# Attention output on one Trainium2 core: one transposition and four 64x64 products in place of two folding products and one full product

## What is computed

```python
x = x + attn(layernorm(x))            # Wq, Wk, Wv, Wo: 128 x 128
x = x + ffn(layernorm(x))             # w_router 128 x 8, w1 8 x 128 x 512, w2 8 x 512 x 128, bias

def attn(x):                          # per head: softmax(q k / sqrt(8)) v over a window of 64
    ...
    ctx = ctx.transpose(0, 2, 1, 3).reshape(Bx, Lx, D_OUT)   # 16 heads x 8 channels side by side
    return ctx @ Wo
```

## Time and profile before

| | |
|---|---|
| three runs, median | 861.02 us (860.0 to 861.64) |
| the profiled execution, own time | 864.88 us |
| its span, first to last instruction | 863.0 us |
| mean granted TensorE clock | 0.951 of full |
| attention and routing of sequences, about | 20 to 535 us |
| experts | 600 to 863 us |
| PE busy, share of the span | 88% |
| DVE, ACT, POOL busy | 60%, 52%, 41% |

### The profile page before, as it was taken

How to read it: one execution, slowest core, us unless ns; L and a number is a source line. 1 busy time by engine, 2 the same in 40 slices (tenths; PEclk the granted TensorE clock), 3 DMA queues, 4 the chain that set the end, 5 groups by cost and what they waited for, 6 DMA issues and landing times. The chain is left out here.

```text
span 863.0 us, 19198 instructions
## 1 busy us (share of the span) xinstructions
PE 760.3 (88%) x7469; PEld 544.6 (63%) x7469; DVE 519.1 (60%) x1623; ACT 451.1 (52%) x923; POOL 357.1 (41%) x318
## 2 busy tenths in 40 slices
PE   7999999999999999999999998427999889889983
PEld 3556666666566566566666555314988778778872
DVE  7888888988888888887887887610222212211210
ACT  5576685585585585585586664202444334334421
POOL 3000000032232222322322343562877877877877
PEclk9999999999999999999999999557999999999997
DMA  4942000010110010010010011113364554554533
GB/s 137 387 160 62 8 15 8 34 33 25 50 33 21 31 47 30 22 56 30 21 57 30 21 66 40 67 51 117 32 111 59 93 101 58 96 97 59 87 31 33
DMA packets 50132, 54.21 MB, mean 63 GB/s; under 512 B 6018, under 2 KB 39449, under 8 KB 49025
## 3 DMA queue, kind: packets, MB, share of 16 engines
q0 software_dynamic: 22528, 17.22, 14.0%
q1 hardware_dynamic: 27520, 35.86, 12.6%
HBM read 17.70 MB, written 31.59 MB: 57 GB/s over the span
## 5 line engine op out<-in xcount | busy, mean ns | idle before, releaser
L445 POOL DMA_INDIRECT out<-y_sb,xg x128 | 199.2, 1556 | 71.1 <-issue 55.0
L363 POOL DMA_INDIRECT slots_dram<-send_rows,slot_id x112 | 110.3, 985 | 229.4 <-PE sT_ps L1135 163.1
L520 ACT ACTIVATE probsT<-sT_ps 128x1024 f32<-128x1024 f32 x128 | 132.4, 1035 | 60.2 <-PE sT_ps L1135 58.7
L687 DVE TRANSPOSE_TENSOR_REDUCE kmax<-sT_ps 128x32 f32<-128x1024 f32 x128 | 159.5, 1246 | 6.2 <-PE sT_ps L1118 5.7
L619 ACT ACTIVATE hT<-sT_ps 128x512 f32<-128x512 f32 x128 | 76.6, 599 | 154.7 <-PE sT_ps L1347 139.1
L1118 PE MATMUL sT_ps<-qbd,kT 64*128 64x256 f32 x1024 | 133.2, 380 | 0.0
L1347 PE MATMUL sT_ps<-xT_hl,w_hl 128*128 128x512 f32 x384 | 105.1, 426 | 24.8 <-DVE xT_hl L1045 18.5
L1055 DVE TENSOR_TENSOR y_sb<-o_ps,xg 128x256 f32<-128x256 f32 x32 | 13.6, 425 | 188.3 <-DMA out<-y_sb,xg 106.2
L1118 PEld LDWEIGHTS sT_ps<-qbd,kT 64*128 64x128 f32 x1024 | 98.6, 191 | 9.8
L1347 PEld LDWEIGHTS sT_ps<-xT_hl,w_hl 128*128 128x128 f32 x384 | 75.9, 204 | 43.9 <-DVE xT_hl L1045 19.1
L380 POOL TENSOR_TENSOR xbias<-x_sb,bias_sb 128x256 f32<-128x256 f32 x32 | 23.5, 734 | 192.8 <-PE sT_ps L1135 192.8
(11 more groups left out here) (171 smaller groups left out, 1124.7 us busy)
## 6 DMA issues: line engine op xcount, KB each, us to landing
slots_dram<-empty_rows SPq DMA_DIRECT2D x8, 1096.0 KB, 16.7
xg<-slots_dram SPq DMA_DIRECT2D x32, 274.0 KB
out<-xbias SPq DMA_DIRECT2D x32, 128.0 KB
w_sb<-in_L_ffn_w SPq DMA_DIRECT2D x16, 256.0 KB
send_rows<-rows_sb SPq DMA_DIRECT2D x7, 548.0 KB, 3.2
out<-y_sb,xg POOLq DMA_INDIRECT x128
slots_dram<-send_rows,slot_id POOLq DMA_INDIRECT x112
out<-empty_rows SPq DMA_DIRECT2D x1, 1024.0 KB, 24.4
```

Of the source, the lines that this page charges most:

```text
L363: pool.indirect_dma_start(out=slots_dram, out_offset=bass.IndirectOffsetOnAxis(ap=slots[:, k, j:j + 1].bitcast(U32), axis=0), in_=rows[:, ...
L445: pool.indirect_dma_start(out=out, out_offset=bass.IndirectOffsetOnAxis(ap=xg[:, r, 4 * c + k, ROW - 1:ROW].bitcast(U32), axis=0), in_=y_s ...
L520: nc.scalar.activation(probsT[:, gp].rearrange("p b k h q -> p (b k h q)"), sT_ps[:, gp].rearrange("p b c -> p (b c)"), ACT.Exp).then_inc( ...
L687: nc.vector.tensor_reduce(kmax[:, u % 2, :], sT_ps[:, u % 2].rearrange("p b (c q) -> p (b c) q", q=32), AX.X, ALU.max, apply_transpose=Tru ...
```

## The change

`normalise` writes even and odd heads into the same 64 columns per block, for two blocks 128 columns without gaps. `context_T` is one transposition of [128, 128]; its result has block and channel in the partitions, and even and odd heads in columns 0 to 63 and 64 to 127. `project` is four products of 64x64 stationary and 128 moving columns: for each block one with the even heads and one with the odd heads, added in PSUM; block 0 uses rows and columns 0 to 63 of the array, block 1 rows and columns 64 to 127. Wo is held twice, in both halves of the partitions, split by even and odd heads. The zeroing of ctx_sb and `fold` go.

```diff
-        wo_sb = sb("wo_sb", [P, D])
+        wo_sb = sb("wo_sb", [P, 2, D])
...
-        ctx_sb = sb("ctx_sb", [P, 2, 2, HP * DH])
-        fold = sb("fold", [P, BLK])
+        ctx_sb = sb("ctx_sb", [P, 2, HP * DH])
...
-            wo4 = wo.rearrange("(j two d) n -> two j d n", two=2, d=DH)
+            wo4 = wo.rearrange("(b g p two d) n -> two g b p d n", b=2, g=2, p=2, two=2)
             for two in range(2):
-                for j in range(HP):
-                    at = two * HP + 4 * (j // 2 % 2) + 2 * (j // 4) + j % 2
-                    sp.dma_start(wo_sb[at * DH:(at + 1) * DH, :], wo4[two, j]).then_inc(ld_w, 16)
+                for at in range(0, P, 16):
+                    b, g = at // 16 % 2, at // STRIP % 2
+                    sp.dma_start(wo_sb[at:at + 16, two, :], wo4[two, g, b]).then_inc(ld_w, 16)
...
-                    last = nc.vector.tensor_tensor(out=ctx_sb[q, :, par, :].rearrange("p b (j d) -> p b j d", d=DH),
+                    last = nc.vector.tensor_tensor(out=ctx_sb[q, :, :].rearrange("p b (j d) -> p b j d", d=DH),
...
-            nc.vector.memset(ctx_sb[:, :, :, :], 0.0)
-            nc.vector.tensor_tensor(out=fold[:, :], in0=ident[:, 0:BLK], in1=ident[:, BLK:P], op=ALU.add)
...
             def context_T(g):
                 pe.wait_ge(s_ctx, g + 1)
-                for blk in range(2):
-                    last = mm(tail_ps[:, blk * BLK:(blk + 1) * BLK], ctx_sb[:, blk, :, :].rearrange("p h c -> p (h c)"),
-                              fold[:, :], start=True, stop=True)
-                last.then_inc(s_ctxT, 1)
+                nc.tensor.transpose(tail_ps[:, 0:P], ctx_sb[:, :, :].rearrange("p b c -> p (b c)"), ident[:, :]).then_inc(s_ctxT, 1)
 
             def project(g):
-                last = mm(tail_ps[:, ATT:ATT + D], ctxT[:, :], wo_sb[:, :], start=True, stop=True)
+                for two in range(2):
+                    for blk in range(2):
+                        rows = slice(blk * HALF, (blk + 1) * HALF)
+                        last = mm(tail_ps[rows, ATT:ATT + D], ctxT[rows, two * BLK:(two + 1) * BLK], wo_sb[rows, two, :],
+                                  start=(two == 0), stop=(two == 1))
                 last.then_inc(s_att, 1)
```

## The result

The changed kernel takes **876.72 us** in the median of four runs (874.24 to 879.43), against 861.33 for the kernel before in the same session (860.0 to 862.56). The ratio is 1.0185, with a 95% interval of 1.0156 to 1.0215: slower by 15.4 us. The forecast was 871.6, slower by 10.6, in a range of 861 to 880. The sign and the range hold; the forecast's own range, 866 to 876, is missed by 0.7 us.

A forecast was written before the change was run, and what follows sets the result against it. PE was the first suspect, each slot a ring of handovers between PE and DVE. Context savings and projection costs net +1.55 us a sequence, +10.6 us in all on 861.0, giving 871.6 us; range 861 to 880.

The forecast's parts named there:

- the forecast's own range: Whole kernel: 866 to 876 us, allowing for slots 4 and 7, cheaper gaps, and one or two more clock falls.
- The context step: End of each slot's second half on PE: one transposition instead of four instructions, 0.33 us sooner, gaining only where PE is late.
- rival 1: Context saving outweighs the projection's added cost x per slot: faster, 852 us at x = 0; chance 0.10.
- The projection: First half of each slot on PE: two rounds of two products, 0.38 us more in odd slots, 0.33 in even ones.
- The sum over the slots: Net of context savings and projection costs over eight slots: +1.55 us a sequence, +10.6 us for the kernel.
- The further change of shape beside `counts` and `router`: Slots 1 and 6, where these full-array products precede `project`: one more change of array shape, 0.2 us in all.
- The slots most in doubt: First halves of slots 4 and 7: unclear whether DVE or PE is late; if DVE, 2.7 us less.
- a sequence of about 66.9 us: Sign that the forecast is right: a sequence's length after the change, against 65.3 us before.
- The loads of Wo: Start of the kernel: 16 loads with twice the bytes, same number of issues; bound 0 to 0.3 us, taken as 0.
- rival 4: Clock falls in slot 6 of six more sequences, 1.3 us each: 8 us, 879 us; chance 0.11.
- rival 3: Projection's two quarters in a round take turns because they write one bank: 23 us more, 895 us; chance 0.07.
- rival 2: No gap between quarters and full array: a slot pays 0.16 us for extra passes, no change, 861 us; chance 0.06.

The follow-up runs named there:

- x3: The kernel before with only the packed context and its one transposition, old projection and loads kept, output wrong: 852.42 us, ratio 0.9895.
- x5: x1 with two full 128x128 projection products instead of four 64x64 ones, as many passes, output wrong: 866.04 us, ratio 1.0026.
- x1: The changed kernel with 16 simple loads of Wo, each 8 partitions of 1 KB lying together in memory, output wrong: 869.62 us, ratio 1.0097.
- x2: The kernel before with only the change's loads of Wo, its one product reading the first table, output wrong: 868.48 us, ratio 1.0083.
- x4: The kernel before with only the four 64x64 projection products, old context step, simple loads of Wo, output wrong: 881.62 us, ratio 1.0255.
- x7: The changed kernel with each of the 16 Wo loads filling 8 partitions with both rows, same result: 873.97 us, ratio 1.0114.
- x8: The changed kernel with x's second half loaded before Wo and PE's wait for weights moved from slot 0 to slot 2: 874.93 us, ratio 1.0109.
- x9: The kernel before with one context transposition and four folding copies on ACT, but the old folding products after slots 3 and 4: 859.28 us, ratio 0.998.

## Why the prediction was right, and where it was not

**The context step: right.** Forecast as 0.33 us less on PE, worth 0.25 in slots 0 and 5, 0.33 in 4 and 6 on the path: 1.16 us a sequence, 8.7 us in all where the projection doesn't change (rival 1 at x = 0). x3 measured 1.09 a sequence and 8.7 in all. The waits for `moving` appeared in slots 0 and 5, as it said.

**The projection: right in size.** Forecast +0.38 in odd slots; slot 3 shows 0.25 to the next group and 0.11 of uncovered weights, 0.36. The forecast's way of checking it ("about 0.7 us to the next group") was worded for the sum, and the row reads 0.58 there, since the weights count behind it. The idle 0.2 on both sides came as said. Its parts come out too: of the 0.36, x5 puts 0.22 on the two further passes and 0.14 on the changes of shape and the uncovered weights, where the forecast had 0.22 and 0.16. The passes are thus the larger part, but the context step pays for nearly all of them: with the same passes in the full array the change would have cost 1.6 us, not 8.5.

**The sum over the slots: slightly too high.** 1.55 us a sequence was forecast, 1.31 measured (x1 against x2), by these first halves and savings (us, from the starts of `shifted` in both):

| slot | 0 | 1 | 2 | 3 | 4 | 5 | 6 | 7 |
|---|---|---|---|---|---|---|---|---|
| forecast | +0.08 | +0.58 | 0 | +0.38 | 0 | +0.13 | 0 | +0.38 |
| first half, x1 - x2 | 0.31 | 0.45 | 0.24 | 0.36 | 0.42 | 0.37 | 0.27 | 0.36 |
| context step ahead of it | -0.24 | 0 | -0.32 | 0 | -0.33 | -0.25 | -0.32 | 0 |
| measured net | +0.07 | +0.45 | -0.08 | +0.36 | +0.09 | +0.12 | -0.05 | +0.36 |

The further change of shape beside `counts` and `router` is worth 0.09 in slot 1 and not 0.2. Slot 2 was taken as paced by DVE, and it is: its first half takes 3.75 us in x1, but also in x3, where the projection is the old one, and 3.65 in x4, against x2's 3.50. So DVE takes back 0.25 of the context's 0.33 there, and the quarters add nothing to that. The slots most in doubt were 4 and 7, and both behave as PE's, but for 0.11 that x3 loses in slot 4. The sign that the prediction named, a sequence of about 66.9 us, did not show as it was worded: the change's full-clock sequence takes 65.97, only 0.64 more than the 65.33 of before, since the kernel before had the slow second half of slot 2 in that profile. In us of the kernel: +10.6 forecast, +8.5 measured by x1, its interval reaching from 5.0 to 11.7.

**The loads of Wo: wrong, and this is the step that failed.** The prediction wrote that "the 16 loads of Wo move twice the bytes, on a queue that the same number of issues fills; bound 0 to 0.3 us" and took 0. They cost 7.1 us (the change less x1) to 7.4 (x2 alone). It counted issues and looked at bytes; what changed was the layout of each load, from 8 partitions to 16, and with it the time of an issue from 0.36 to 0.67 us, while PE's wait ahead of slot 0 and DVE's for x stood at the end of that queue. The rows for it were in the trace of before: SP's row of 5.70 us for 16 issues, and DVE's wait of 0.47 us for x behind it. With a wait there already, the bound should have been at least the doubling of that row, 0 to 5.7 us, and the range 5 us wider at the top. The two parts measured apart, x1's 8.5 and x2's 7.4, make 15.9 against the 15.4 measured: no further cost need be hidden in the difference.

That 876.7 still lies within 861 to 880 is luck. The upper end was set by rival 4, six further falls of the clock, and the loads' 7 us fell into the room that was left for it.

**The rivals.** *Quarters that take turns* (rival 3) is false. The eight instructions in slot 3 start in four pairs, the first two at 315.939 and 315.946, then 316.099 and 316.106, with the results of both quarters in one bank, and the eight leave the array nearly as soon as x5's four, which need no sharing: 0.58 us to the next group against 0.54. The Trainium skill says in TensorEngine Tiling (Array Packing), Gotcha 1, that different row tiles cannot access the same PSUM bank at the same time; this trace doesn't agree for two tiles that differ in their rows and in their columns: the starts lie 0.007 us apart, not a stream of 0.11. *The context wins* (rival 1) and *no gap* (rival 2) fell with the 0.58, 0.20 and 0.17 of the rows. Rival 2 had its own number too low: it put the two further passes at 0.16 us a slot, where its 0.11 for a pass makes 0.22, as x5 shows; x5 is that rival built, and it is 1.6 us slower, not even. *The clock* (rival 4) happened in part: in slots 6 three falls in the profile after where one was before, not six more. At 1.4 to 1.9 us each the two further ones are 2.7 to 3.7 us of that one execution. The median doesn't hold them: the change's four runs have a mean granted clock of 0.945 to 0.950, 0.948 on average, and the kernel before has 0.949 to 0.950 on average in the three sessions of the experiments. One fall of 3.4 us takes 1.7 / 877 = 0.002 off that mean, by my estimate, so there is room for about one further fall in the median, not for the 8 us of the rival. Nor do the falls go with the kernel: x1 and x7, with the same instructions in their slots as the change, have one each in their slots 6 in the profile, x8 with them too has four, and so has x9, which has no quarters.

## What to carry to other kernels

Before a projection of the engines, read each load that the change rewrites as an issue: how long one takes by the row of its queue, whether its layout stays the same, and what stands behind it on that queue that the first tiles wait for. A group of products in another shape of the array costs two changes and the uncovered weights of what follows, here 0.14 us a slot beyond its passes; it must remove more than that from the same engine. And a saving is worth what the next waiter leaves of it: 8.7 us for the context step alone, nothing when the folding moved to copies that PE then waited for.

## What the runs showed of the hardware

- **The time to issue a load depends on its layout, not on its bytes.** 16 loads: 5.70 us at 8 partitions of 512 B each (before), 5.70 at 8 partitions of 1 KB (x1), 5.69 at 8 partitions with two pieces of 512 B (x7), 10.74 at 16 partitions of 512 B (x2, after). It is not the number of partitions alone: one load of 512 B into each of 128 partitions took 0.43 us to issue (Wk, before), one of 16 partitions 0.67.
- **The issue right behind the large load of x holds the queue.** It took 8.66 us where that was the first load of Wo (x8), and 8.89 where it was the first store to slots_dram (before). No run isolates the reason.
- **Two 64x64 products in opposite quarters run side by side into one bank**, started 0.007 us apart.
- **DVE can lose 2 us to a fill by POOL.** A copy of 128x2 elements took 2.15 us instead of 0.16 while POOL's memset of 128x2192 ran for 1.93 us. Two profiles show it for this copy, those of the change and of x9; the others have the like for a later copy of DVE (L853 before, 1.71 us against 0.44). It was not tried by itself, and it makes a profiled start some 2 us early or late without any edit.
- **Half clock came in slots 6**, 3.4 us at a time, in a number that doesn't follow the kernel: three sequences in the profile of the change, one each in x1's and x7's and four in x8's with the same slots, four in x9's, one before. No run isolates the reason.
